# Cross attention of a two-layer perceiver: a deeper ring of keys, two more probability buffers, a head's output four key-tile pairs later

## What is computed

```
x = x + L0_xattn(ctx, ctx, layernorm(x), mask, Wv, Wk, Wq, Wo, bo)
...
x = x + L1_xattn(layernorm(x), ctx, ctx, ..., Wq, Wk, Wv, Wo, bo)

def xattn(q, k, v):                      # 16 heads of 32, 512 queries, 8192 keys
    energy = einsum('nqhd,nkhd->nhqk', q, k)
    energy = where(mask == 0, -1e20, energy)     # layer 0 only
    attention = softmax(energy * scale, axis=3)
    out = einsum('nhql,nlhd->nqhd', attention, v).reshape(n, q_len, 512)
    return out @ Wo.T + bo
```

## Time and profile before

| | |
|---|---|
| median of 3 runs | 4753.92 us (4748.25 to 4754.37) |
| the profiled execution | 4741.35 us, span 4739.6 us |
| busy share of the span | PE 87%, DVE 64%, ACT 45%, POOL 44% |
| mean granted TensorE clock | 0.92 of full |
| layer 0 cross attention, heads | about 490 to 1600 us of the span |
| layer 1 cross attention, heads | about 2750 to 3830 us of the span |

### The profile page before, as it was taken

The page is one execution under the profiler, slowest core; times in us unless marked ns, Lnnn a source line. Parts: engine busy times, 40 slices in busy tenths (PEclk is TensorE's granted clock), DMA queues, the critical chain, the costliest instruction groups (busy, mean ns, idle before and its releaser), DMA issues. The chain is left out here.

```text
span 4739.6 us, 50995 instructions
## 1 busy us (share of the span) xinstructions
PE 4103.6 (87%) x17384; PEld 2236.5 (47%) x17384; DVE 3035.5 (64%) x5059; ACT 2130.9 (45%) x2348; POOL 2068.5 (44%) x1208
## 2 busy tenths in 40 slices
PE   8995999999999686689999588888888879669997
PEld 6883444443434251157777343333333323347775
DVE  4335777777777259945777476666766543377776
ACT  2220444554545333324767145455555623146675
POOL 0000788888889616400000168778887920000000
PEclk9996999999999779889999789899998979889998
DMA  8997565665655300024888468778887840307876
GB/s 299 338 330 257 125 141 128 142 144 128 142 136 131 102 13 0 0 82 154 303 302 311 146 144 186 174 176 186 175 190 179 179 111 0 99 9 281 304 301 234
DMA packets 294006, 803.62 MB, mean 170 GB/s; under 512 B 47475, under 2 KB 81011, under 8 KB 256372
## 3 DMA queue, kind: packets, MB, share of 16 engines
q1 hardware_dynamic: 223764, 561.77, 34.7%
q0 software_dynamic: 61280, 221.80, 23.3%
q10 hardware_dynamic: 8704, 16.78, 1.1%
HBM read 485.81 MB, written 98.37 MB: 123 GB/s over the span
## 5 line engine op out<-in xcount | busy, mean ns | idle before, releaser
L588 PE MATMUL psum<-k_ring,q_stack 98*128 98x512 f32 x2048 | 916.5, 471 | 218.6 <-DMA k_ring<-k_lo 132.9
L858 POOL TENSOR_TENSOR den_pool<-den_pool,prob 128x1024 f32<-128x1024 f32 x418 | 1022.2, 2445 | 146.4 <-ACT prob L698 128.0
L698 ACT ACTIVATE prob<-psum 128x1024 f32<-128x1024 f32 x726 | 741.9, 1024 | 697.1 <-PE psum L610 658.5
L744 DVE TENSOR_REDUCE row_max<-psum 128x1 f32<-128x512 f32 x1024 | 682.5, 689 | 326.8 <-PE psum L588 322.6
L748 DVE CUSTOM_DVE_ANT_0 psum<-psum,mask_q 128x512 f32<-128x512 f32 x1024 | 703.1, 707 | 291.4 <-PE psum L588 289.7
L610 PE MATMUL psum<-q_stack,k_ring 98*128 98x512 f32 x2048 | 884.3, 504 | 2.8 <-ACT prob L698 2.5
L588 PEld LDWEIGHTS psum<-k_ring,q_stack 98*128 98x128 f32 x2048 | 409.2, 200 | 932.7 <-issue 339.0
L1814 DVE TENSOR_TENSOR weight_lo<-weight_raw,weight_hi 128x2048 fp32r<-128x2048 f32 x240 | 547.0, 2290 | 162.2 <-ACT weight_hi L1757 161.9
L858 POOL TENSOR_TENSOR den_pool<-den_pool,xnT 128x1024 f32<-128x1024 f32 x190 | 465.0, 2447 | 62.2 <-ACT xnT L698 52.3
L1757 ACT ACTIVATE weight_hi<-weight_raw 128x2048 fp32r<-128x2048 f32 x240 | 453.9, 1915 | 39.3 <-DMA weight_raw<-in_L_ffn_w 22.4
L698 ACT ACTIVATE xnT<-psum 128x1024 f32<-128x1024 f32 x298 | 304.7, 1024 | 297.6 <-PE psum L610 276.8
(11 more groups left out here) (398 smaller groups left out, 6354.1 us busy)
## 6 DMA issues: line engine op xcount, KB each, us to landing
den_dma<-prob POOLq DMA_DIRECT2D x254, 512.0 KB, 5.0
weight_raw<-in_L_ffn_w SPq DMA_DIRECT2D x120, 1024.0 KB, 6.5
k_ring<-k_hi SPq DMA_DIRECT2D x1024, 64.0 KB, 2.7
weight_raw<-in_L_ffn_Wu SPq DMA_DIRECT2D x60, 1024.0 KB, 7.1
weight_raw<-in_L_ffn_Wd SPq DMA_DIRECT2D x60, 1024.0 KB, 5.0
den_dma<-xnT POOLq DMA_DIRECT2D x98, 512.0 KB, 4.9
k_ring<-k_lo SPq DMA_DIRECT2D x512, 64.0 KB, 2.6
den_pool<-den_dma POOLq DMA_DIRECT2D x48, 512.0 KB, 5.6
```

The costliest lines, as they stand in the source:

```text
L588: e.matmul(k.bank(maxbank[i % 2]), q_stack[h % n_q][:, i * P:(i + 1) * P], k_ring[:, n % KRING, :], start=True, stop=True).then_inc(s_max, 1)
L698: e.activation(prob[g % n_p], k.psum[:, 2 * j2:2 * j2 + 2, :], ACT.Exp, scale=scale).then_inc(s_exp, 1)
L744: e.reduce_max(out, bank, AXIS_X).then_inc(s_red, 1)
L858: e.tensor_tensor(den[:], den[:], tile, ALU.add).then_inc(s_dpool, 1)
```

## The change

Five edits, all in `cross_attention`; every other function is as it was.

1. The ring of keys is sized per layer: `kring` = NKC + LEAD + 3 = 20 slots in layer 0 and NKC + LEAD + 15 = 32 in layer 1, where both had 19. Each chunk still comes by three loads, one for each of its three copies, as before.
2. Layer 1 has 10 tiles of probabilities where it had 8; layer 0 keeps 6.
3. `head_out` and `head_rows` go from p = 8 to p = 12, and `den_sum` with `divide_four` from p = 11 to p = 15.
4. The buffer `small` is gone. ACT writes the high part of the row maximum straight into the two rows of `q_stack`, and DVE works on it in place; two waits that went with it are dropped.
5. The bias row lies in `den_pool[0]`. Its load moves from chunk 1 of the last head to the end of SP's list, behind a wait for the output of head 14.

```diff
-KRING = NKC + LEAD + 2
...
-    n_q, n_p = 3, 6 if masked else 8
+    n_q, n_p = 3, 6 if masked else 10
+    kring = NKC + LEAD + (3 if masked else 15)
...
-    k_ring = k.sbuf(ctx, "k_ring", [QROWS + 2, KRING, KC], F32R)
+    k_ring = k.sbuf(ctx, "k_ring", [QROWS + 2, kring, KC], F32R)
...
-    small = k.sbuf(ctx, "bias_and_m_hi", [QROWS + 2, T], F32)
-    bias_row, m_hi = small[0:1, :], small[rows_m, :].bitcast(F32R)
+    bias_row = den_pool[0][0:1, 0, :]
...
-                if n >= KRING:
-                    e.wait_ge(s_score, 2 * (n - KRING) + 2)
+                if n >= kring:
+                    e.wait_ge(s_score, 2 * (n - kring) + 2)
...
-            for n in range(KRING):
+            for n in range(kring):
                 load_k(n)
             load_q(1)
             load_v(0)
             for n in range(NCH):
                 h, c = divmod(n, NKC)
-                if n + KRING < NCH:
-                    load_k(n + KRING)
+                if n + kring < NCH:
+                    load_k(n + kring)
...
                     e.dma_start(v_first[:], w_out).then_inc(s_wo, 16)
-                    e.dma_start(bias_row, bias).then_inc(s_bo, 16)
                 elif c == 1:
                     load_v(h + 1)
+            e.wait_ge(s_head, H - 1)
+            e.dma_start(bias_row, bias).then_inc(s_bo, 16)
             e.wait_ge(s_wave, WAVES * H)
...
-                if p == 8 and h > 0:
+                if p == 12 and h > 0:
                     head_out(h - 1)
...
             def m_hi_rows(h):
                 e.wait_ge(s_topT, h + 1)
-                if h > 0:
-                    e.wait_ge(s_mlo, h)
-                e.activation(m_hi, misc[rows_m, :], ACT.Copy).then_inc(s_mhi, 1)
+                e.activation(q_stack[h % n_q][rows_m, :], misc[rows_m, :], ACT.Copy).then_inc(s_mhi, 1)
...
-                if p == 8 and h > 0:
+                if p == 12 and h > 0:
                     head_rows(h - 1)
...
                 e.wait_ge(s_mhi, h + 1)
-                if h >= n_q:
-                    e.wait_ge(s_score, reused_stack(h))
-                e.scalar_tensor_tensor(out=q_stack[h % n_q][rows_m, :], in0=small[rows_m, :], scalar=lo_sign[rows_m, :],
+                m_rows = q_stack[h % n_q][rows_m, :]
+                e.scalar_tensor_tensor(out=m_rows, in0=m_rows.bitcast(F32), scalar=lo_sign[rows_m, :],
...
-                if p == 11 and h > 0:
+                if p == 15 and h > 0:
                     den_sum(h - 1)
...
-            for n in range(KRING):
+            for n in range(kring):
                 e.memset(k_ring[rows_m, n, :].bitcast(F32), -1.0).then_inc(s_ring, 1)
-            e.wait_ge(s_ring, n_q + KRING)
+            e.wait_ge(s_ring, n_q + kring)
```

More of the change, by code:

```diff
@@ L501, in cross_attention @@
     o_sb = k.sbuf(ctx, "o_sb", [P, T], F32)
-    s_k = [k.sem("s_k") for _ in range(KRING)]
+    s_k = [k.sem("s_k") for _ in range(kring)]
     s_v = [k.sem("s_v") for _ in range(2)]
@@ L540, in load_k @@
                 rows = slice(h * DH, (h + 1) * DH)
-                if n >= KRING:
-                    e.wait_ge(s_score, 2 * (n - KRING) + 2)
+                if n >= kring:
+                    e.wait_ge(s_score, 2 * (n - kring) + 2)
                 for g, part in enumerate((0, 0, 1)):
-                    e.dma_start(k_ring[g * DH:(g + 1) * DH, n % KRING, :].bitcast(F32),
-                                k_hi_lo[part][rows, chunk_cols(c)]).then_inc(s_k[n % KRING], 16)
+                    e.dma_start(k_ring[g * DH:(g + 1) * DH, n % kring, :].bitcast(F32),
+                                k_hi_lo[part][rows, chunk_cols(c)]).then_inc(s_k[n % kring], 16)
             def load_v(h):
@@ L581, in maxima @@
                         e.wait_ge(s_zero, h - n_q + 1)
-                    if n < KRING:
+                    if n < kring:
                         e.wait_ge(s_ring, n_q + n + 1)
-                    e.wait_ge(s_k[n % KRING], 48 * (n // KRING + 1))
+                    e.wait_ge(s_k[n % kring], 48 * (n // kring + 1))
                 if 4 * n + i >= 2:
                     e.wait_ge(s_red, 4 * n + i - 1)
-                e.matmul(k.bank(maxbank[i % 2]), q_stack[h % n_q][:, i * P:(i + 1) * P], k_ring[:, n % KRING, :],
+                e.matmul(k.bank(maxbank[i % 2]), q_stack[h % n_q][:, i * P:(i + 1) * P], k_ring[:, n % kring, :],
                          start=True, stop=True).then_inc(s_max, 1)
@@ L609, in scores @@
                         e.matmul(k.bank(kt), k.ident_big[:], masks[1][:, 2 * p + j, :], start=True, stop=False)
-                    ins = e.matmul(k.bank(kt), k_ring[:, n % KRING, kt * P:(kt + 1) * P], q_stack[h % n_q][:],
+                    ins = e.matmul(k.bank(kt), k_ring[:, n % kring, kt * P:(kt + 1) * P], q_stack[h % n_q][:],
                                    start=not masked, stop=True)
```

## The result

| | before | after |
|---|---|---|
| median of the runs | 4754.15 us (4748.25 to 4754.44, 4 runs) | 4615.03 us (4608.23 to 4622.19, 4 runs) |
| span of the profiled execution | 4739.6 us | 4606.5 us |
| mean granted TensorE clock | 0.92 | 0.93 |

The ratio is 0.971, with a 95% interval of 0.9693 to 0.9728: 139 us less, where 164 were forecast. 4615 lies in the range and 25 us above the predicted 4590. The profiled executions are 133 us apart.

What follows compares the result with a forecast made beforehand. PE was taken to bound both layers, held up by late keys and merges; 127 us from layer 1 and 38 from layer 0, with small ends, made 164 us, so 4577 us profiled and 4590 us predicted, range 4562 to 4660.

Steps and rivals of the forecast that it cites:

- What bounds the kernel: Attention of both layers: PE is the bound; undisturbed heads take 66.3 us in layer 0 and 56.6 us in layer 1.
- The ring: Key loads in both layers: more slots take nearly all key waits away, with 48 us of lead in layer 1.
- the second rival: Layer 0: one more chunk is not enough, so it gives 10 us instead of 38; 4618 us, chance 0.08.
- The failed-ring rival: Key loads: engines deliver late all the time, so every wait returns and only 30 us are gained; 4724 us, chance 0.03.
- slower by landings: Layer 1 denominators: DMA landings decide from 8.4 us on; a mean of 9.5 us gives 4816 us, chance 0.03.
- `head_out` at p = 12: Layer 1 output, four pairs (6.8 us) later: the second merge, 2.2 us late on average at p = 8, should make it.
- The division: After every fourth head DVE is held and PE stands for 4.58 us, counted as 1.0 us per head.
- POOL comes late next: Layer 1: POOL needs 58.1 us per head, half a us above PE's floor, so 58.5 us were taken.
- the last head: End of layer 1: it ends with POOL and its two merges, entered a little later, counted as minus 3 us.
- The signs: Profile after: no key or merge waits, layer 1 maxima 58 to 59 us apart, clock 0.97, POOL over 90% busy.
- The tiles, the maximum in place, the prologue: Ten tiles, the row maximum's edit and filling the ring at layer 1's start: worth nothing, the filling hidden.
- The Trainium skill's rule on the shared 16 engines: Layer 1 loads from SP and GpSimd share engines, but 54 us of DMA work per head does not bind.

## Why the prediction was right, and where it was off

**What bounds the kernel: right.** The floor in layer 0 was 66.3 us by the sum; undisturbed heads now take 66.3 to 66.4. In layer 1 it was 56.6, and they take 56.2.

**The ring: right, and more than was needed.** Key waits went in both layers, and layer 0 with one further slot has 1.7 us of them left, against the second rival. The 48 us of lead in layer 1 are not what helps: two chunks, some 7 us, do it. The failed-ring rival is out, and so is "slower by landings": DMAs into `den_dma` land in 5.6 us in the median, not 8.4.

**`head_out` at p = 12: the step that failed.** The text took four pairs, 6.8 us, against a wait of 2.2 us on average and a landing of 9.0 at most, which leaves 4.6 us to spare, and concluded that the merges make it. The average was misread: of its 30.2 us, 11.5 are the last wait of the stage and 6.2 that of head 15, and heads 1 to 14 waited 0.9 us each. Above all it was a wait of a PE that late keys held back, and of two merges in a row. Counted from the head's first exponential, the second merge lands after 18.9 us with the ring alone, and PE with keys on time asks after 13.8 us at p = 8 and after 20.6 at p = 12. The wait at p = 8 would thus have been 5 us (the ring alone shows it) and the spare time is 1.7 us, not 4.6. Where POOL enters a head 2 to 3 us late and its first merge meets the values, that is too little: five heads, 21 us. At p = 16 it is gone.

**The division: mis-sized.** The sum had 4.58 us a division, PE's idle time alone. The whole cost, with the slow pair behind it, was already 6.1 to 6.8 us in the profile before, and is 8.2 to 8.8 in layer 1 and 7.5 to 8.3 in layer 0 now, where POOL adds more densely and the product waits for its adds. That is 1.8 us a head of layer 1 in place of 1.0, and it is why layer 0 came to 68.0 and not 67.7.

**"POOL comes late next": right in kind.** 58.1 us by its own work was not a floor: with all of POOL's adds, heads 1 to 14 of layer 1 take 57.1 us where the division is taken apart. The 0.9 us a head that the sum gave away for it went to `head_out` and p = 31 instead. By terms: 56.2 + 1.8 (divisions) + 1.5 (`head_out`) + 0.6 (p = 31) = 60.1 us, the measured head, against 58.5.

**The balance.** 164 us were forecast and 133 came in the profiled spans. Missing are 22 in the first 15 heads of layer 1, 5 in layer 0, and 8.5 that no term had: the three stretches outside both loops became longer by 1.5 + 3.4 + 3.6 us. Such differences are no more than what these stretches vary by. The part behind the second cross attention is the same code in every kernel here, and it took 886.7 to 895.5 us in the 14 profiled executions; the kernel before had the lowest of them and the changed one 888.1. Partly against this, the last head did not lose 3 us but gave 1.5. By the profiled executions the kernel is 31 us over the forecast of 4577. The 12.5 us between profiled execution and median were no property of the kernel either, they are 7 us after, and so 4615 is only 25 over 4590.

**The signs.** Met were the key waits, the clock (0.97 over layer 1's heads) and the landings into `den_dma` under 6 us; ACT waits 1.1 us for `den_dma` there. Not met were the copies of the row maximum (60.1 us apart, not 58 to 59) and `head_out` without a wait, and the sign of POOL (over 90%) was met in one of the two stretches shown.

**The tiles, the maximum in place, the prologue: right** at nothing. The Trainium skill's rule on the shared 16 engines (DMA: Bandwidth & Descriptors, section Issuing engines are not separate DMA queues) was no bound, as the prediction had it: at a share of 0.93 PE ran a head in 56.2 us once GpSimd's adds were small.

## What to carry to other kernels

When one wait is removed, take the time at which every engine asks and at which every transfer lands anew, counted from one common event, at the pace that the kernel will have: two waits that lie side by side cover each other, and the repairs one by one (65 and 20 us) give less than both together (139). Give a prefetch one more slot before giving it thirteen. And cut a long operation into pieces only if the pieces meet nothing: what must wait for another engine's add waits once per piece.

## What was new about the hardware

- VectorE beside GpSimd's adds of 128x1024: a product of 128x512 with two SBUF inputs took 0.69 us alone, 1.05 in layer 1 before and 2.3 to 2.96 after; a copy of 128x4 took 0.17 us alone and up to 3.2. The adds themselves took 2.38 us in the median in layer 1 before, 2.72 after and 3.0 in the fastest kernels. A reciprocal of 128x512 (3.35 us), reductions of SBUF (0.22 us) and those of PSUM (0.69 us) took the same in every kernel.
- An adding DMA of 512 KB into `den_dma` landed in 5.1 to 5.8 us in the median of layer 1 in every kernel, whatever GpSimd's load. A merge took 5.2 to 7.0 in the median and up to 11.3, those of 10 us and more where the 1 MB of values was issued within 1 us of it; with the values elsewhere 6.9 was the longest.
